# Two heads' scores from the two halves of the array, without staged copies, in a graph network on one core

## The reference

```python
h = jnp.maximum(_layernorm(x, axis=-1), 0.0)
q = h @ wq.T + bq                 # k and v alike, and then once more:
q2 = (q @ wiq.T + biq).reshape(N, H, D).transpose(1, 0, 2)
scores = jnp.einsum('hnd,hmd->hnm', q2, k2) * scale + mask[None]
attn = jax.nn.softmax(scores, axis=-1)
out = jnp.einsum('hnm,hmd->hnd', attn, v2)
x = x + out.transpose(1, 0, 2).reshape(N, OUT_F) @ wo.T + bo
```

## Time and profile before

| | us |
|---|---|
| three runs, median | 1011.81 |
| lowest and highest of them | 1007.88, 1015.37 |
| the profiled execution | 1011.11 |
| its span in the trace | 1009.4 |
| PE busy, of the span | 953.7 (94%) |
| DVE busy | 633.2 (63%) |
| POOL busy | 459.9 (46%) |
| ACT busy | 370.3 (37%) |

### The profile page before, as it was taken

One profiled execution on the slowest core, in us unless ns is written; L12 is line 12 of the kernel. 1 busy time (PEld: TensorE's weight loads), 2 busy tenths in 40 slices (PEclk: granted clock), 3 DMA queues, 4 the chain that ended last, 5 costly groups with the idle time before them and its releaser, 6 DMA issues.

```text
span 1009.4 us, 13566 instructions
## 1 busy us (share of the span) xinstructions
PE 953.7 (94%) x4695; PEld 832.3 (82%) x4695; DVE 633.2 (63%) x991; ACT 370.3 (37%) x583; POOL 459.9 (46%) x407
## 2 busy tenths in 40 slices
PE   3999999999999979999999999999999969999994
PEld 3999999995677968888888888888888848877883
DVE  5898888865896354656466555565646465445625
ACT  5333333344775344323222232222324334234321
POOL 5334444466555203547475474754758103115322
PEclk8999999997998989999999999999999979999997
DMA  8998766643665453344434444343333523323301
GB/s 212 202 270 232 204 159 171 158 102 59 110 115 126 130 193 117 113 128 126 155 101 154 134 128 153 99 149 105 105 116 114 171 72 115 112 98 105 125 21 62
DMA packets 94913, 134.35 MB, mean 133 GB/s; under 512 B 35512, under 2 KB 72592, under 8 KB 94864
## 3 DMA queue, kind: packets, MB, share of 16 engines
q1 hardware_dynamic: 77760, 129.32, 43.6%
q0 software_dynamic: 15584, 0.11, 3.7%
q10 hardware_dynamic: 1520, 4.30, 1.2%
HBM read 116.65 MB, written 7.59 MB: 123 GB/s over the span
## 4 chain that ended last, share of the span: by engine, by line
PE 88%; DVE 5%; DMA 3%; ACT 1%; issue 1%; POOL 1%; SPq 1%; ACTq 0%; DVEq 0%; POOLq 0%
PE ps L593 47%; PE ps L445 23%; PE ps L640 8%; PE ps L547 2%; PE ps L508 2%; PE ps L507 2%; DMA rel_r<-acts 1%; PE ps L422 1%; PE ps L518 1%; DVE stats L1043 1%; SPq L339 1%; DMA weight_d<-weight_sum,cell 1%; DMA e_in<-in_edge_type 1%; PE ps L433 1%; PE ps L744 1%
## 5 line engine op out<-in xcount | busy, mean ns | idle before, releaser
L1166 DVE TENSOR_TENSOR wlo<-raw,whi 128x1024 fp32r<-128x1024 f32 x120 | 207.2, 1730 | 136.3 <-ACT whi L829 136.2
L445 PE MATMUL ps<-acts,whi 128*128 128x384 f32 (+1 forms) x896 | 230.7, 338 | 3.7 <-DVE acts L1139 3.7
L1521 POOL TENSOR_TENSOR mean_lo<-mean_f,mean_hi 128x384 fp32r<-128x384 f32 x80 | 92.7, 1158 | 191.8 <-ACT mean_hi L962 191.8
L445 PEld LDWEIGHTS ps<-acts,whi 128*128 128x128 f32 x896 | 162.4, 189 | 3.8 <-issue 3.8
L962 ACT ACTIVATE mean_hi<-mean_f 128x384 fp32r<-128x384 f32 x80 | 42.0, 525 | 300.2 <-DVE mean_f L1286 300.2
L445 PE MATMUL ps<-acts,wlo 128*128 128x384 f32 (+1 forms) x448 | 150.6, 336 | 0.0
L593 PE MATMUL ps<-whi,mean_hi 128*128 128x512 f32 x480 | 149.5, 392 | 0.9 <-POOL mean_lo L1521 0.9
L593 PE MATMUL ps<-whi,mean_lo 128*128 128x512 f32 x480 | 148.8, 391 | 0.0
L593 PE MATMUL ps<-wlo,mean_hi 128*128 128x512 f32 x480 | 148.7, 391 | 0.0
L829 ACT ACTIVATE whi<-raw 128x1024 fp32r<-128x1024 f32 x120 | 125.4, 1048 | 21.7 <-PE ps L593 21.7
L1542 POOL DMA_INDIRECT weight_d<-weight_sum,cell x48 | 95.6, 1991 | 31.1 <-DMA weight_d<-weight_sum,cell 20.7
(11 more groups left out here) (172 smaller groups left out, 1504.8 us busy)
## 6 DMA issues: line engine op xcount, KB each, us to landing
raw<-in_L_gnn_weight SPq DMA_DIRECT2D x64, 512.0 KB, 3.3
rows_b<-rows_d SPq DMA_DIRECT2D x24, 384.0 KB, 5.3
raw<-in_L_gnn_w_gate SPq DMA_DIRECT2D x16, 512.0 KB, 3.4
raw<-in_L_gnn_W_self SPq DMA_DIRECT2D x16, 512.0 KB, 3.3
raw<-in_L_gnn_W_neigh SPq DMA_DIRECT2D x16, 512.0 KB, 3.3
rel_r<-acts SPq DMA_DIRECT2D x64, 96.0 KB
count_d<-total_r SPq DMA_DIRECT2D x8, 576.0 KB, 5.3
rel_r<-count_d SPq DMA_DIRECT2D x8, 576.0 KB, 4.6
```

The costliest lines, as they stand in the source:

```text
L445: mm = pe.matmul(ps[:, j % 2, 0:N], stationary[j % RING][:, k, :], acts[:, a, moving, k, :], start=i == 0, stop=i == 3 * KT - 1)
L1166: dve.tensor_tensor(wlo_row[slot], raw[slot][:, :], whi_row[slot].bitcast(F32), ALU.subtract)\
L1521: pool.tensor_tensor(mean[1][:, k % 2, :], mean_f[:, k % 2, :], mean[0][:, k % 2, :].bitcast(F32), ALU.subtract).then_inc(S["mean_lo"], 1)
```

## The change

1. **Scores.** `stage_scores` is gone, with its semaphores. `scores(pair, nt)` makes one block of scores for both heads: six matmuls of 64 rows, alternately from the upper and the lower 64 rows of `acts`, into two neighbouring banks. Banks 0 and 1 serve blocks 0 and 2, banks 2 and 3 block 1.
2. **Turned probabilities** share two banks, 4 and 5, in turn. `turn_probs(o, m)`, `probs_high(o, m)` and `probs_low(o, m)` are now single blocks, woven between the scores of the next pair and the products with v. Scores of four heads are held (`sc`): two in `xres`, two in `sc_more`, which lies in the place of the staged q and k.
3. **Sums.** `invert_sums` takes the reciprocal of three columns (`rinv`) and then copies it spread (`rinv_cols`).
4. **Output pairs.** `o_f` has a place for each pair, in `rows_b`. The low parts of pairs 0 to 6 are made by POOL, between its scatters of counts (`PAIR_AFTER`), the last one by DVE (`last_lo`).
5. **SP** issues only `stage_v` in attention; `relation_counts` waits in addition until the probabilities are turned and the pairs are made.
6. **Start.** DVE makes all statistics and the first two shifts ahead of the wait for the edges; PE turns the edges between blocks 1 and 2 of x, and DVE copies `e_col` between the low parts of the second block and the two halves of the third.

```diff
+        PAIR_AFTER = (19, 21, 25, 27, 31, 33, 37)
-            stage_v(0)
-            stage_v(1)
-            for o in range(2, H):
-                stage_scores(o)
-                if o >= 4:
-                    stage_v(o - 2)
-            stage_v(H - 2)
-            stage_v(H - 1)
+            for o in range(H):
+                stage_v(o)
...
+            def scores(pair, nt):
+
+                if pair:
+                    pe.wait_ge(S["scores_read"], 6 * pair + (0, -2, 2)[nt])
+                elif nt == 0:
+                    pe.wait_ge(S["v_made"], KT)
...
+                for n, (a, c) in enumerate(((0, 0), (0, 1), (1, 0))):
+                    for e in range(2):
+                        d = slice(DH * e, DH * e + DH)
+                        mm = pe.matmul(ps[:, 2 * (nt % 2) + e, 0:N], acts[d, 0, a, pair, P * nt:P * nt + P],
+                                       acts[d, 1, c, pair, :], start=n == 0, stop=n == 2)
+                        if n == 2:
+                            mm.then_inc(S["scores_ready"], 1)
+
+            def turn_probs(o, m):
+                pe.wait_ge(S["exp_ready"], 6 * (o // 2) + 5 + o % 2)
...
+                    pe.wait_ge(S["pt_lo"], o * NT + m - 1)
                 for nt in range(NT):
...
+                    mm = pe.transpose(ps[:, 4 + (o * NT + m) % 2, P * nt:P * nt + P],
+                                      sc[o % 4][:, nt, P * m:P * m + P], ident[:, :])
+                mm.then_inc(S["probs_turned"], 1)
...
+            for pair in range(H // 2):
+                e, o = 2 * pair, 2 * pair + 1
+                turn_probs(e, 0)
+                turn_probs(e, 1)
+                if o + 1 < H:
+                    scores(pair + 1, 0)
+                    scores(pair + 1, 1)
+                if pair:
+                    weigh_values(e - 1)
+                turn_probs(e, 2)
+                turn_probs(o, 0)
+                spread_sums(pair)
+                if o + 1 < H:
+                    scores(pair + 1, 2)
+                turn_probs(o, 1)
+                turn_probs(o, 2)
+                weigh_values(e)
             weigh_values(H - 1)
...
             def invert_sums(o):
-                dve.wait_ge(S["exp_ready"], (o + 1) * NT)
                 d0 = DH * (o % 2)
-                dve.reciprocal(rinv[:, o // 2 % 2, :, d0:d0 + DH],
-                               rsum[:, o % 2, :].unsqueeze(2).to_broadcast([P, NT, DH])).then_inc(S["sum_inverted"], 1)
+                dve.wait_ge(S["exp_ready"], 6 * (o // 2) + 5 + o % 2)
+                link(dve.reciprocal(rinv[:, o % 2, :], rsum[:, o % 4, :]))
+                dve.tensor_copy(rinv_cols[:, o // 2 % 2, :, d0:d0 + DH],
+                                rinv[:, o % 2, :].unsqueeze(2).to_broadcast([P, NT, DH])).then_inc(S["sum_inverted"], 1)
...
+            def pair_low(pair):
+                pool.wait_ge(S["pair_hi"], pair + 1)
+                pool.tensor_tensor(acts[:, 0, 1, pair, :], o_f[:, pair, :], acts[:, 0, 0, pair, :].bitcast(F32),
+                                   ALU.subtract).then_inc(S["pair_lo"], 1)
+
             for c in range(EC):
                 add_counts(c)
+                if c in PAIR_AFTER:
+                    pair_low(PAIR_AFTER.index(c))
```

More of the change, by code:

```diff
@@ L69, in build @@
         mask = sb("mask", [P, NT, N], F32)
+        with ExitStack() as scope:
+            sc_more = sb("sc_more", [P, 2, NT, N], F32, scope)
         rel_r = sb("rel_r", [P, 2, NT, N], F32R)
@@ L534, in weigh_values @@
                 pair, e = divmod(o, 2)
-                if e:
-                    spread_sums(pair)
-                elif pair:
+                if e == 0 and pair:
                     pe.wait_ge(S["pair_made"], pair)
-                else:
+                elif e == 0:
                     pe.wait_ge(S["v_lo"], KT - 1)
@@ L567, in pair_ready @@
                 if k == KT - 1:
[L568 removed]
+                    pe.wait_ge(S["last_lo"], 1)
             def turn_y(j):
@@ L901, in probs_high @@
+            def probs_high(o, m):
                 need(act, S["pv_done"], o - 1)
-                for m in range(NT):
-                    act.wait_ge(S["probs_turned"], o * NT + (m + 1))
-                    act.activation(pt[0][:, o % 2, m, :], ps[:, NT + m, 0:N], ACT.Copy).then_inc(S["pt_hi"], 1)
+                act.wait_ge(S["probs_turned"], o * NT + (m + 1))
+                act.activation(pt[0][:, o % 2, m, :], ps[:, 4 + (o * NT + m) % 2, 0:N], ACT.Copy)\
+                   .then_inc(S["pt_hi"], 1)
@@ L915, in _ @@
             v_high(KT - 1)
-            exps(0)
-            exps(1)
-            for o in range(H):
-                probs_high(o)
-                if o + 2 < H:
-                    exps(o + 2)
-                if o % 2 and o > 1:
-                    pair_high(o // 2 - 1)
-                elif o > 1:
-                    read_spread(o // 2 - 1)
-            read_spread(H // 2 - 1)
+            for nt in range(NT):
+                exp(0, nt)
+                exp(1, nt)
+            for pair in range(H // 2):
+                e, o = 2 * pair, 2 * pair + 1
+                more = o + 1 < H
+                probs_high(e, 0)
+                probs_high(e, 1)
+                if more:
+                    exp(e + 2, 0)
+                    exp(o + 2, 0)
+                    exp(e + 2, 1)
+                probs_high(e, 2)
+                probs_high(o, 0)
+                if more:
+                    exp(o + 2, 1)
+                probs_high(o, 1)
+                probs_high(o, 2)
+                if more:
+                    exp(e + 2, 2)
+                    exp(o + 2, 2)
+                read_spread(pair)
+                if pair:
+                    pair_high(pair - 1)
@@ L1072, in start_stats @@
                 norm_stats(0, nt)
-            start_stats(0)
+            for nt in range(NT):
+                start_stats(nt)
+                if nt < NT - 1:
+                    norm_shift(0, nt)
             dve.wait_ge(S["edges_in"], 16 * 4)
@@ L1144, in _ @@
             turn_tile(0, 0)
-            for n in range(len(START)):
-                start_low(n)
+            start_low(0)
+            start_low(1)
+            dve.wait_ge(S["edges_turned"], 1)
+            dve.tensor_copy(e_col[:, :, :], ps[:, 0, 0:4 * EC].rearrange("p (f c) -> p f c", f=4))\
+               .then_inc(S["edge_cols"], 1)
+            start_low(2)
+            start_low(3)
             dve.wait_ge(S["h_ready"], len(START))
@@ L1255, in _ @@
-            pair_low(H // 2 - 2)
+            invert_sums(1)
+            for pair in range(H // 2):
+                e, o = 2 * pair, 2 * pair + 1
+                more = o + 1 < H
+                if more:
+                    score_max(e + 2, 0)
+                    score_max(o + 2, 0)
+                    score_max(e + 2, 1)
+                probs_low(e, 0)
+                probs_low(e, 1)
+                if more:
+                    score_max(o + 2, 1)
+                if pair:
+                    make_pair(pair - 1)
+                probs_low(e, 2)
+                probs_low(o, 0)
+                if more:
+                    score_max(e + 2, 2)
+                probs_low(o, 1)
+                if more:
+                    score_max(o + 2, 2)
+                probs_low(o, 2)
+                if more:
+                    invert_sums(e + 2)
+                    invert_sums(o + 2)
@@ L1256, in _ @@
             make_pair(H // 2 - 1)
-            pair_low(H // 2 - 1)
+            dve.wait_ge(S["pair_hi"], H // 2)
+            dve.tensor_tensor(acts[:, 0, 1, H // 2 - 1, :], o_f[:, H // 2 - 1, :],
+                              acts[:, 0, 0, H // 2 - 1, :].bitcast(F32), ALU.subtract).then_inc(S["last_lo"], 1)
             def add_y(j):
```

150 lines of the change are left out of this document (49 added, 101 removed).

## The result

Five runs of the kernel after took 1003.12 us in the median (1001.05 to 1003.57), five of the kernel before 1010.23. The ratio is 0.9917, with a 95% interval of 0.989 to 0.9944: a gain of 7 to 8 us where 16 were forecast.

What follows compares the result with a forecast made beforehand. PE's attention work plus 22 us of staging-copy waits was taken as the bound. Attention ending at 308 instead of 325.0 gives 17.0 us, less 1 for clock: 16 off 1011.1, so 995, range 986 to 1007.

Steps and rivals of the forecast that it cites:

- within 1% of before: Whole kernel: a time that a measurement cannot tell from no change, about 10 us either way; chance 0.21.
- rivals 2 and 3: Attention: halves neither overlap nor drain, 1000 to 1006, chance 0.13; queue order and two banks stretch pairs, 1003 to 1008, 0.11.
- bounds for POOL: End of POOL's seventh pair_low: 303 us without the loads' disturbance, 311 if scatters run as late as before plus loads.
- The end of PE's own attention work: Attention on PE: scores start at 227.4, first turn 232.7, seven pairs at 8.7 us, end 302.5, with low clock 306.
- The low clock: Beginning of attention: PE idles through most of 5.3 us, then one stretch at half clock adds 3.4 us.
- The halves: Score products: two 64-row products on separate halves cost 0.174 us together, plus 0.2 per entry or exit, four times per head pair.
- rival of the small products: Scores: each 64-row product still costs 0.37 us, PE takes 12.4 us a pair, kernel 1018 to 1022; chance 0.06.
- The first product: Start: PE begins at about 20.8 us, released by POOL's low half of weight tile 0; gain 1.4, bounds 0 to 3.4.
- POOL's seventh pair_low: End of attention: PE's wo product waits for it behind scatter 37; it ends at 307.6 us, bounds 303 and 311.
- The disturbance: POOL's scatters late in attention: loads of wo and x stretch one landing, adding 4.7 us before scatter 36 at 302.8.
- PE's resuming: Start of the wo product: PE resumes at 308 us against 325.0 before, with 1 us given back to low clock.
- Nothing behind attention late: After attention: remaining scatters end near 345 us, before their counts are needed, so nothing there becomes late.

## Why the prediction came out as it did

**Forecast 995, measured 1003.1.** The value lies in the range of 986 to 1007 and misses the forecast by half of the gain. It is also within 1% of before, a case that the forecast had given 0.21. It is where the rivals 2 and 3 had put it (1000 to 1008), with the mechanism of neither: the halves overlap, and the pair of heads did not stretch. That it lies in the range at all is in part luck, as an error of 7 us at POOL was not covered by the bounds for POOL. Its steps, one by one:

- *The end of PE's own attention work* was forecast for 306, with 3.4 us of low clock in it, and is 302.74. That the sum without the clock, 302.5, comes so near is chance. The first turn stands at 234.01 instead of 232.7. The low clock came where it was expected, from 235 to 241.8, but its 3.4 us had no row behind them. The first pair, from its scores for the next pair (234.89) to the same place a pair later (245.01), took 10.1 us, 1.7 more than the later ones with clock and waits together; the forecast had 8.7 + 3.4, 2.0 too much. Six more pairs took 8.38 us each instead of 8.7, another 1.9 less, and the first turns and the last stretch were 0.5 shorter. So 3.9 + 0.5 less, and 1.3 for the later beginning, make up the difference to 306.
- *The halves.* They overlap, as assumed, and no rival of the small products came true. The price was right, 0.174 a pair of products and 0.2 four times: for entering in the group itself (0.72 = 3 x 0.174 + 0.2), for leaving in the row behind it (nine products with v 1.77 instead of 1.57, six turns 0.82 instead of twice 0.33). Only the turns were charged twice for leaving, since the 1.13 of the earlier trace rows had it already. By these pieces a pair is 1.57 + 0.77 + 6 x 0.33 + 0.33 + 3.14 = 7.8 us of work; the other 0.6 of the 8.38 stand in turns that wait (six took 0.98, three 0.52).
- *The first product* was forecast for 20.8 and came at 21.11, with the releaser named (POOL's `wlo`). But the 1.4 us of gain were not there. The bound named for that was 0 "if the edge rows, now finished 1.3 us later, delay weight tile 1"; the mechanism was of that kind, one tile further on: tile 2 lands late and the mask stands behind it. The bound was too mild: with the old start and early edges the products ended 1.65 us sooner. And the earlier trace rows showed the edges landing late. The five profiled executions with the old start had them at 7.8 to 9.9 us, and PE began 12.3 to 12.4 us behind that, at 20.2 to 22.2; the nine with the new start began at 20.9 to 21.1. Against 20.2 to 20.6 (three of the five) there is nothing to gain. The ends of the weight products say the same: 226.4 to 226.7 us with the old start and early edges, 228.0 and 228.15 with late ones, 227.7 to 229.1 with the new start in its seven executions, and 226.1 and 226.5 with the new start and the mask first.
- *POOL's seventh pair_low* was forecast to end at 307.6, with bounds of 303 and 311, and ended at 314.34, beyond both. This is the step that failed. Scatter 36 was put at 302.8 and came at 309.82, 7.0 us later: 1.4 since scatter 10 did not move with the start (226.34 in both), 4.8 since 12 pairs took 72.4 us instead of 67.6 (2.7 of them at the `pair_low` that waited 3.73 us for ACT; that it "fits into the 2.2 us that POOL waits there anyway" holds for its work, not for its wait; 1.2 more in the last pair ahead of scatter 34, which before had been as slow, 7.3 us without any `pair_low`, and the 12 pairs together had taken 70.2 there), and 0.8 since the stretched landing cost 5.5 us instead of 4.7. The disturbance itself was rightly foreseen; that it goes when the reload of x is moved was shown. How much the late pair_lows cost on their own is not settled: with the first four put later, scatter 36 still started at 309.38.
- *PE's resuming.* With PE ready at 302.74 and POOL at 314.34, the gap is 11.7 us where the forecast had 2. Behind so long a gap the clock is low for the first turns and the first column: 1.94 + 6.03 instead of 0.87 + 4.17, that is 2.9 us, all by which the output product is longer. The forecast gave 1.
- *Nothing behind attention late* held: from the end of the output product to the end of the span it is 643.4 us in both.

The balance of the span: 0.1 (start) + 22.1 (PE's own attention work) - 11.7 (gap) - 2.9 (clock) = 7.6, as measured. With the gap taken away (`pair_low` behind scatter 35) the kernel takes 992, 3 us below the forecast. The Trainium skill, "TensorEngine Tiling (Array Packing)", Key Properties, says that different tiles can multiply in parallel, and the run on one half (2.28 against 1.25 us) agrees with it.

## What to carry to other kernels

When work of a few hundred ns to 2 us moves to an engine that issues and waits for DMAs, its price is the landing it comes to stand behind: look at which DMAs will be in flight when the critical engine wants the result, and put it ahead of that wait. Try the smallest part of a change by itself; here the removed staging alone gave 16.6 us of a best total of 22, and the whole change 7. And read a start that follows a DMA's landing from more than one execution, since that landing moved by 2 us from one to the next.

## What the runs showed of the hardware

- Two matmuls of 64 rows on the two halves of the array ran side by side at 0.174 us a pair in both orders tried: three of the upper and then three of the lower half took 0.73 us, the alternation 0.72. On one half six take 1.24. Going from 128-row to 64-row work cost 0.2 us, and going back cost another 0.2, which shows in the row behind (1.77 instead of 1.57).
- Scatters of 128 single values, 5.5 us a pair, took 11.1 with a reload of 1.5 MB issued between the two (7.3 to 10.9 in other runs, where it was issued at another distance from them), and 5.5 with the loads of wo (512 KB each) on SP beside them and the reload behind them.
- After 11.7 us of standing still PE's granted clock was 0.50 for the next 5.8 us (6.03 us for a column), after 8.3 us as well (6.05). After 11.3 us in another run it was low for 3.2 us only (4.82). After 2.8 us it was not low (4.17).
